# Query features in two halves, the hidden activations scaled on ScalarE alone, and a new order of weight subtractions on VectorE, in a one-core graph layer with experts

## The reference

```python
xn = layernorm(x)
x = x + gnn(xn, edges, W, b) + mix(xn, W_qkv, W_proj, b_proj, proj_mat)
x = x + ffn(layernorm(x), gate_w, ..., fc1_w, fc1_b, ln_w, ln_b, fc2_w, fc2_b)

# mix, for each of 12 heads; q, k, v are 625 x 64, proj_mat is 266 x 64
dd = (q / 64**.25) @ proj_mat.T
q1 = 266**-.5 * (exp(dd - |q|**2 / 16 - dd.max(row)) + 1e-4)     # k1: max over all of k
out = (q1 @ (k1.T @ v)) / (q1 @ k1.sum(0))

# ffn: expert 0 takes every token, each token has up to 3 of the others
h = gelu(xf @ fc1_w[e] + fc1_b[e])                 # 768 -> 1536
h = (h - mean) * rsqrt(var + 1e-5) * ln_w[e] + ln_b[e]
y = h @ fc2_w[e] + fc2_b[e]                        # 1536 -> 768
out = sum over e of combine[:, e] * y
```

## Time and profile before

| | |
|---|---|
| median of 3 runs | 1316.48 us (1313.85 to 1317.22) |
| the profiled execution | 1310.28 us |
| its span in the trace | 1308.6 us |
| mean granted clock of TensorE | 0.981 |
| TensorE busy | 1229.3 us, 94% |
| VectorE busy | 847.8 us, 65% |
| ScalarE busy | 665.0 us, 51% |
| GpSimd busy | 245.9 us, 19% |

### The profile page before, as it was taken

The page is one execution under the profiler, slowest core; times in us unless marked ns, Lnnn a source line. Parts: engine busy times, 40 slices in busy tenths (PEclk is TensorE's granted clock), DMA queues, the critical chain, the costliest instruction groups (busy, mean ns, idle before and its releaser), DMA issues.

```text
span 1308.6 us, 22128 instructions
## 1 busy us (share of the span) xinstructions
PE 1229.3 (94%) x7041; PEld 1092.1 (83%) x7069; DVE 847.8 (65%) x1465; ACT 665.0 (51%) x990; POOL 245.9 (19%) x184
## 2 busy tenths in 40 slices
PE   4899999999997989999999999999999999999985
PEld 3899998998585766789888889988889988889875
DVE  5676666606426855666378686675686698755993
ACT  3313233326614641442466677375577576666853
POOL 1000000003004010005323242121252243213301
PEclk7999999999997999999999999999999999999998
DMA  9100000000005033310686668356659786576944
GB/s 324 40 1 1 1 1 1 1 1 24 2 1 184 2 121 105 109 24 14 194 302 207 223 232 320 108 222 208 214 218 321 250 313 221 174 264 221 336 161 111
DMA packets 55395, 188.97 MB, mean 144 GB/s; under 512 B 7626, under 2 KB 8260, under 8 KB 55346
## 3 DMA queue, kind: packets, MB, share of 16 engines
q1 hardware_dynamic: 47858, 170.07, 35.0%
q0 software_dynamic: 6448, 17.91, 6.7%
q10 hardware_dynamic: 1040, 0.33, 0.1%
HBM read 176.70 MB, written 14.51 MB: 146 GB/s over the span
## 4 chain that ended last, share of the span: by engine, by line
PE 70%; DVE 13%; issue 5%; DMA 4%; DVEq 3%; ACT 3%; ACTq 1%; SPq 0%; POOL 0%; POOLq 0%
PE bank L1812 19%; PE bank L1796 16%; PE bank L1523 7%; PE bank L1611 4%; PE bank L1593 4%; DMA w1raw<-in_L_ffn_fc_w 3%; PE bank L1633 3%; PE bank L1646 2%; DVE w1lo L505 2%; DVEq L519 2%; DVE w2lo L505 2%; PE bank L1665 2%; PE bank L1780 2%; PE bank L1692 2%; PE bank L1733 2%
## 5 line engine op out<-in xcount | busy, mean ns | idle before, releaser
L505 DVE TENSOR_TENSOR w2lo<-w2raw,w2hi 128x1536 fp32r<-128x1536 f32 x96 | 165.6, 1754 | 40.8 <-ACT w2hi L492 40.4
L492 ACT ACTIVATE w2hi<-w2raw 128x1536 fp32r<-128x1536 f32 x96 | 142.2, 1507 | 96.1 <-DMA w2raw<-in_L_ffn_fc_w 83.7
L1812 PE MATMUL bank<-w2hi,hthi 128*128 128x384 f32 x624 | 162.6, 341 | 11.0 <-DVE htlo L1070 10.3
L1812 PE MATMUL bank<-w2lo,hthi 128*128 128x384 f32 x624 | 159.5, 336 | 0.0
L1812 PE MATMUL bank<-w2hi,htlo 128*128 128x384 f32 x624 | 159.2, 336 | 0.0
L492 ACT ACTIVATE w1hi<-w1raw 128x1536 fp32r<-128x1536 f32 x96 | 139.2, 1507 | 34.2 <-DMA w1raw<-in_L_ffn_fc_w 34.2
L1523 PE MATMUL bank<-ohd,ohs 125*125 125x313 bf16 x825 | 129.5, 305 | 20.9 <-DVE ohd L845 19.7
L505 DVE TENSOR_TENSOR w1lo<-w1raw,w1hi 128x1536 fp32r<-128x1536 f32 x80 | 136.9, 1778 | 7.6 <-ACT w1hi L492 7.6
L745 POOL DMA_INDIRECT out<-ysb,sidx x27 | 88.8, 3288 | 281.3 <-issue 241.2
L1796 PE MATMUL bank<-w1hi,xthi 128*128 128x512 f32 x486 | 139.7, 396 | 0.0
L1796 PE MATMUL bank<-w1lo,xthi 128*128 128x512 f32 x486 | 136.9, 390 | 0.0
(11 more groups left out here) (306 smaller groups left out, 2019.5 us busy)
## 6 DMA issues: line engine op xcount, KB each, us to landing
w1raw<-in_L_ffn_fc_w SPq DMA_DIRECT2D x96, 768.0 KB, 6.8
w2raw<-in_L_ffn_fc_w SPq DMA_DIRECT2D x96, 768.0 KB, 6.3
wg<-in_L_gnn_W SPq DMA_DIRECT2D x1, 2304.0 KB, 13.7
wv<-in_L_mix_W_qkv SPq DMA_DIRECT2D x1, 2304.0 KB, 20.0
wk<-in_L_mix_W_qkv SPq DMA_DIRECT2D x1, 2304.0 KB, 24.8
wq<-in_L_mix_W_qkv SPq DMA_DIRECT2D x1, 2304.0 KB, 24.5
out<-xs SPq DMA_DIRECT2D x5, 375.0 KB
xn_dram<-xn SPq DMA_DIRECT2D x5, 375.0 KB
```

The source lines that it names most:

```text
L492: act.activation(unit(w2hi if second else w1hi, second, u), unit(w2raw if second else w1raw, second, u), ACT.Copy).then_inc(w2_hi if secon ...
L505: eng.tensor_tensor(unit(w2lo if second else w1lo, second, u), unit(w2raw if second else w1raw, second, u), unit(w2hi if second else w1hi, ...
L1812: last = pe.matmul(y_ps[s][:, 0:384], a[:, c, :], w[:, c, 384 * s:384 * s + 384], start=c == 0 and k == 0, stop=False)
```

## The change

Ten edits in the programs of the engines:

1. VectorE's `hidden_scale` is gone; ScalarE scales all 12 chunks. The semaphore `v_scaled_act` goes, `v_scaled` is ScalarE's.
2. In the expert loop, VectorE subtracts w2 unit 3 before `hidden_low(j)`, w2 units 4 and 5 behind it, and w1 units 4 and 5 of the block that step j's `fc1` works on behind those (`with_first(dve, j - 1, ...)`). Units 1 to 3 stay in the step before, mixed with w2 units 0 to 2.
3. `q_features` works on six heads at a time; the first half of tile 0 comes after head 7 of the `kv` copies. TensorE waits for half a tile at a time.
4. The tail of the query features is transposed before pair 3, and its product closes each group of heads where it opened it; TensorE no longer waits for its own last product there.
5. The key features of the last tile come before the last messages of the graph part, and TensorE waits for key features tile by tile.
6. The five bias pieces are all done after tile 3 and within tile 4.
7. Most of GpSimd's constants are written after the last graph product, the rest after the last `kv`.
8. The first layer output is stored before the loads of w2 units 3 to 5, and units 4 and 5 are loaded after the last stores.
9. `project_out(2)` comes before `turn_xn2(0)`.
10. w2 unit 4 of expert 0 is subtracted before `normalise(1)`.

```diff
@@ VectorE, expert loop
             with dve.Fori(FIXED, end) as j:
-                hidden_scale(j, entry(dve, EXPERT, j - 1, E - 1))
-                with_second(dve, j, low(3, 4))
+                with_second(dve, j, low(3))
                 hidden_low(j)
-                with_second(dve, j, low(5))
+                with_second(dve, j, low(4, 5))
+                with_first(dve, j - 1, low(4, 5))
                 normalise(j)
                 x_low(j + 1)
-                with_first(dve, j, low(1, 2, 3, 4, 5))
-                with_second(dve, j + 1, low(0, 1, 2))
-            hidden_scale(end, entry(dve, EXPERT, end - 1, E - 1))
-            with_second(dve, end, low(3, 4))
+                with_first(dve, j, low(1, 2))
+                with_second(dve, j + 1, low(0, 1))
+                with_first(dve, j, low(3))
+                with_second(dve, j + 1, low(2))
+            with_second(dve, end, low(3))
             hidden_low(end)
-            with_second(dve, end, low(5))
+            with_second(dve, end, low(4, 5))
+            with_first(dve, end - 1, low(4, 5))
             normalise(end)
-            hidden_scale(nb, E - 1)
@@ ScalarE
-            def hidden_scale(j, e, first=SCALE_BY_ACT):
+            def hidden_scale(j, e):
 
                 act.wait_ge(h_turned, j)
-                for c in range(first, FC):
+                for c in range(FC):
                     last = act.activation(hid[:, 128 * c:128 * c + 128], tr_ps[c // 4][:, 128 * (c % 4):128 * (c % 4) + 128],
                                           ACT.Identity, scale=lnw[:, bass.ds(e, 1), c], bias=lnb[:, bass.ds(e, 1), c])
-                last.then_inc(v_scaled_act, 1)
+                last.then_inc(v_scaled, 1)
@@ VectorE, query features and bias pieces
-            def q_features(i):
-                for h in range(H):
+            def q_features(i, g):
+                heads = slice(6 * g, 6 * g + 6)
+                for h in range(6 * g, 6 * g + 6):
                     taken(dve, ("ddq", i, h))
-                main = q1[i % 2][:, :, 0:MAIN]
+                main = q1[i % 2][:, heads, 0:MAIN]
@@
-                    if p == 4 and i + 1 < NT:
-                        q_features(i + 1)
-                    if p == 5:
-                        bias_part(i)
+                    if p in (2, 4) and i + 1 < NT:
+                        q_features(i + 1, p // 4)
+                    if i == NT - 1 and p in (0, 1, 3):
+                        bias_part((1, 3, None, 4)[p])
@@
+                if i == NT - 2:
+                    bias_part(0)
@@ VectorE, key features
+            for i in range(NT - 1):
+                add_messages(i)
+                k_features(i)
+            k_features(NT - 1)
+            add_messages(NT - 1)
@@ TensorE
                 for i in range(NT):
+                    if g == 0:
+                        pe.wait_ge(k1_ok, i + 1)
@@
                 if p % 3 == 2:
-                    filled(last, ("o", i, g))
-                    done(pe, ("o", i, g))
-                    pe.sem_inc(q1t_used, 1)
-                else:
-                    last.then_inc(q1t_used, 1)
+                    taken(pe, ("tail", i))
+                    filled(pe.matmul(ps[0:TP, 0:6 * (HD + 1)], q1tt[:, i % 2, :], kvt[:, 6 * g:6 * g + 6, :], start=False, stop=True), ("o", i, g))
@@
-                pe.wait_ge(q1_ok, i + 1)
+                pe.wait_ge(q1_ok, 2 * i + 1)
                 turn_pair(i, 0)
@@
+                    if p == 2:
+                        pe.wait_ge(q1_ok, 2 * i + 2)
@@
             project_out(1)
+            project_out(2)
             turn_xn2(0)
-            project_out(2)
```

More of the change, by code:

```diff
@@ L332, in gps_kernel @@
         for i in range(NT):
-            groups([("q1t", i, 0), ("tail", i)], R6)
+            groups([("q1t", i, 0)], R6)
             for p in range(H // 2):
@@ L336, in gps_kernel @@
                     groups([("q1t", i, p + 1)], R6)
+                if p == 2:
+                    groups([("tail", i)], R6)
                 if i + 1 < NT:
@@ L599, in _ @@
                 sp.wait_ge(x1_ok, i + 1)
+                sp.dma_start(out[TP * i:TP * i + TP, :], xs[:, i, :]).then_inc(st_x1[i], 16)
                 if i == NT - 1:
-                    for u in range(3, C):
-                        load(True, 0, u)
-                sp.dma_start(out[TP * i:TP * i + TP, :], xs[:, i, :]).then_inc(st_x1[i], 16)
+                    load(True, 0, 3)
                 sp.wait_ge(xn2_ok, i + 1)
                 sp.dma_start(xn2_dram[TP * i:TP * i + TP, :], xn2[:, i, :]).then_inc(st_xn2[i], 16)
+            for u in (4, 5):
+                load(True, 0, u)
             sp.wait_ge(st_slot, 16 * TOPK * NT)
@@ L707, in _ @@
                                    base=-32 * g, pattern=[[-1, E], [0, 128]], channel_multiplier=1).then_inc(sel_ok, 1)
+            done(pool, ("kv", H - 1))
+            pool.memset(bl[:, :], 0.0).then_inc(bl_zero, 1)
+            pool.memset(padrow[0:1, :], 0.0).then_inc(pad_ok, 1)
             pool.wait_ge(bsplit_ok, 1)
@@ L955, in _, with add_messages @@
             dve.wait_ge(x_biased, NT + 1)
-            for i in range(NT):
+            def add_messages(i):
                 for s in range(2):
@@ L961, in _, with k_features @@
                                                      op0=ALU.mult, op1=ALU.add), ("gnn", i, s))
+            def k_features(i):
                 dve.wait_ge(kexp_ok, i + 1)
@@ L1058, in _ @@
             STEPS = 11
-            def hidden_scale(j, e, chunks=SCALE_BY_ACT):
-                dve.wait_ge(h_turned, j)
-                for c in range(chunks):
-                    last = dve.tensor_scalar(hid[:, 128 * c:128 * c + 128], tr_ps[c // 4][:, 128 * (c % 4):128 * (c % 4) + 128],
-                                             lnw[:, bass.ds(e, 1), c], lnb[:, bass.ds(e, 1), c], ALU.mult, ALU.add)
-                last.then_inc(v_scaled, 1)
             def hidden_low(j, hi=hthi, lo=htlo):
@@ L1187, in _ @@
             scores()
+            split_lo(dve, True, 0, range(4, 5))
             normalise(1)
-            split_lo(dve, True, 0, range(4, 5))
             x_low(2)
@@ L1377, in _ @@
                         take_pair(i, p + 1)
+                    if p == 2:
+                        take_tail(i)
                     for r in AHEAD[p] if i + 1 < NT else ():
@@ L1681, in attend @@
                 g = p // 3
-                if p % 3 == 0:
-                    ps = fill(pe, ("o", i, g))
-                    taken(pe, ("tail", i))
-                    pe.matmul(ps[0:TP, 0:6 * (HD + 1)], q1tt[:, i % 2, :], kvt[:, 6 * g:6 * g + 6, :], start=True, stop=False)
-                ps = bank[plan[("o", i, g)][0]]
+                ps = fill(pe, ("o", i, g)) if p % 3 == 0 else bank[plan[("o", i, g)][0]]
                 taken(pe, ("q1t", i, p))
@@ L1876, in turn_last @@
                 pe.wait_ge(v_scaled, end)
-                pe.wait_ge(v_scaled_act, end)
                 turn_h(nb)
```

40 lines of the change are left out of this document (17 added, 23 removed).

## The result

The changed kernel takes **1387.6 us** (median of four runs, 1384.3 to 1393.5) against 1315.2 (four runs): ratio **1.0555**, 95% interval 1.0514 to 1.0596. It is 5.5% slower. The forecast was 1367 with a range of 1345 to 1389: the direction and the mechanism are right, the size is 21 us short. The profiled execution of the changed kernel took 1386.6 us, 76.3 more than that of the kernel before (1310.3), where +50.8 was forecast.

A forecast was written before the change was run, and what follows sets the result against it. TensorE, busy 94%, was taken as the bound. Loop +65.6 and first half with end -14.8 gave +50.8 on the profiled 1310.3, so 1361; the median's 6.2 made it 1367 us, range 1345 to 1389.

The forecast's parts named there:

- The mechanism: Expert loop: w1 units 4 and 5, wanted sooner, queue behind later-wanted `htlo` on in-order VectorE; some 15 TensorE waits on `w1lo`.
- T+9.67: T is a loop step's start on TensorE; w1 unit 4 of `fc1` was forecast to begin costing at T+9.65.
- Small steps: Eight expert-change steps with w1 units alone: unit 4 ready at T+11.2, TensorE loses 1.55 us each, 12.4 in all.
- Large steps: Seven steps with w1 and w2 units: TensorE loses 7.4 to 9.9 us each, taken as 8.0, 56 in all.
- s-T: Delay from step start to ScalarE's scaling start in the seven steps: 1.73 us least, 4.24 worst, 3.1 average.
- The clock: TensorE's lower clock behind the seven waits of 8 us costs 1.5 us each, 10.5 in all.
- First half: Before the expert loop: shorter feature and projection waits against costlier bias pieces, -15.5 us in sum.
- Removed waits: Expert loop: the seven old `htlo` waits go, -10.3 us, with -3.0 of their clock.
- The rule weighed: ScalarE's scaling by the skill's fixed-cost figure: an estimated 0.25 us per chunk, not 0.343; sum 17 lower, 1350.
- no small wait was hidden: Rival in the expert loop: eight small waits hidden, seven large stay at 6 to 7 us; 1344 to 1350, 14%.
- the cascade: Rival: later w1 use delays loads, roundings and scaling, small waits slow the clock; 20 to 30 us more, 1385 to 1397, 11%.
- unit 4 is never late: Rival in the expert loop: w1 unit 4 comes in time, only the removals count; 1288 us, 4%.

The follow-up runs named there:

- Experiments 1: Changed kernel with VectorE's w1 units 4 and 5 moved ahead of the w2 unit and `htlo` in the same step: 1285.5 us, ratio 0.9774 to the kernel before.
- 3: Changed kernel with all five VectorE w1 units in the step before, as in the old order; ScalarE keeps all scaling: 1291.7 us, ratio 0.9824.
- 2: Changed kernel with w1 units 4 and 5 still behind `htlo`, but ahead of w2 units 4 and 5: 1355.4 us.
- 5: Kernel before with VectorE's new order of weight units alone, VectorE still scaling four of twelve chunks: 1372.8 us, ratio 1.0451.
- experiment 7: Changed kernel with 34 useless matmuls in TensorE's queue ahead of w1 unit 4 in steps with both weight changes: 1384.1 us.
- Experiment 8: Changed kernel with 50 useless matmuls in TensorE's queue ahead of w1 unit 4 in steps with both weight changes: 1374.1 us.
- experiments 6: Kernel before with the expert loop's change alone (VectorE's new order and ScalarE's scaling), first half as before: 1397.1 us, ratio 1.0638.
- 10: Changed kernel with w1 units 4 and 5 ahead of `htlo`, bias pieces spread over tiles, last w2 unit 5 behind the norm: 1287.1 us, ratio 0.9800.

## Why the prediction was right, and where it was short

- **The mechanism** held as written: `w1lo` as releaser of `fc1`, 15 times, seven large and eight small, `htlo` gone, 27.73 us for a step without a change of expert. Unit 4 begins to cost at T+9.67 (forecast 9.65). Experiments 1 and 3 take the waits away; 2 and 5 move them in the way and near the amounts that it gives (the large ones by 3.0 where 3.4 was expected, the small ones by 1.25 where 1.4 was).
- **Small steps**, 1.55 each: mis-sized, 2.43. The step "start of `htlo`, + 1.67" took VectorE's operations as back to back. Between `htlo` and `w1lo` lies the skipped block of the w2 units, with 0.70 us of "issue"; experiment 2 takes it from between them and the wait is 0.78 shorter. The restart adds 0.3, and `htlo` came 0.1 sooner than forecast.
- **Large steps**, 8.0 each: 9.2. I had 8.8 from the mean of ScalarE's starts and took 8.0, since pauses of TensorE should let the transfers catch up. They did not: s-T is 2.35 to 4.52 in the seven, 3.3 on average, and ScalarE's roundings of w2 still wait for their data ahead of the scaling. From s on the chain is as forecast: in step 25, 3.78 + 5.7 makes 9.5, and the wait is 9.39. The choice within the bounds was wrong. The mean held in the bounds (7.4 to 9.9); the longest single one, a wait of 10.12 and 0.3, did not.
- **The clock**, 1.5 for each large wait: 2.1. I took it from two rows, behind waits of 2.2 and 3.4 us. It varies from 1.3 to 2.8, and not with the length of the wait: 1.3 behind 8.44 us in the changed kernel, 2.8 behind 5.44 in experiment 2, and 1.6 to 2.7 behind the 2.8 to 4.4 of experiment 7. Experiment 8 confirms the mean. Leaving the small waits without it was nearly right: one of eight had it.
- **First half**, -15.5: -9.7 in this profile. Part of the difference was lost to the clock between 190 and 236 us, where nothing was changed. The same first half in the profile of version 1 started step 4 at 614.15, a gain of 13.2, which is 3.5 more. The bias pieces cost 4.65 (a wait of 3.66 where it was 1.29, and 5.67 for the transposes behind it where they took 3.39), where the term was 4.1.
- **Removed waits**, -13.3: -15.1, with their restarts of nearly 0.3 each.
- **The rule weighed**: the chunks came every 0.343 us again (twelve in 4.12 us, from 1281.13 to 1285.25, where the next operation starts), as the earlier trace rows said. The sum by the Trainium skill's figure (VectorE: DVE Perf Modes, The TRN2 errata) would have missed by 38 us.
- **Rivals**: no small wait was hidden. The number falls into what I gave for the cascade (1385 to 1397, 11%), and part of it came true: s-T averaged 3.3. But nothing grew from step to step, since steps without a change of expert take 27.73 behind a large one too, and one small wait of eight slowed the clock. The case "unit 4 is never late" is what experiment 1 made of it: it gave 1288, and that version runs in 1285.5.
- **The median**: I added 6.2 us, because the profiled execution of the kernel before lay that far below its median. The changed kernel's profiled execution lies 1 us below its own; such an offset does not carry over. Without it the forecast would have been 27 us short, not 21: a third of the effect was missing. That the measured time still lies in the range, 1.4 us below its end, owes something to this offset.

## What to carry to other kernels

An in-order queue should be sorted by when the result is wanted, and an operation that itself waits for something late belongs behind whatever it could hold up: VectorE was only 59% busy, and the two units fitted into the 6.7 us for which it stood waiting. When work is moved to another engine, see what is queued behind the operation that it makes later; the same move cost nothing in one order and 24 us in the other. And price a wait of TensorE with what follows it, here 0.3 us of restart and, behind the waits of 2.8 to 10 us in the loop, some 2 us of lower clock.

## What the runs showed of the hardware that I had not expected

- **VectorE and GpSimd hold each other up.** A subtraction of 128x1536 takes 1.75 us on VectorE and 3.5 on GpSimd. Where the two overlap, VectorE's takes up to 5.08 us. In version 1, VectorE and then GpSimd:

```profile
1209.49 6.75 DVE L505 TENSOR_TENSOR w2lo<-w2raw,w2hi 128x1536 fp32r<-128x1536 f32 x2
...
1211.05 3.56 POOL L505 TENSOR_TENSOR w1lo<-w1raw,w1hi 128x1536 fp32r<-128x1536 f32 x1 [1.44 <-PE bank L1789]
```

  The second of the two started at 1211.16 and ended 1.6 after GpSimd's end, as if it had begun only then. It goes the other way too: where VectorE's subtractions are under way first, GpSimd's takes up to 5.04 us in the changed kernel (at 1039.87, beside VectorE's from 1038.11 on). In the loop of the kernel before, no VectorE subtraction took more than 1.76 and none of GpSimd's more than 3.53: the two never met. The Trainium skill (GPSIMD Engine Reference, Specifications) says that GpSimd shares its SBUF interfaces with VectorE, and that instructions with two SBUF inputs contend; the trace agrees.
- **Which waits cost the clock.** It fell behind all seven waits of 8 to 10 us, behind the seven of 4.3 to 7.2 in experiment 2, behind the six of 2.8 to 4.4 that the first filling left, behind one of the eight of 2.1 in the changed kernel, two of eight in experiments 6 and 7 and three of eight in experiment 8, and behind none of 1.33 (experiment 2) or 0.86 (experiment 5). Filling only a part of a wait did not keep the clock up.
- **A skipped conditional block** costs VectorE 0.70 us in the trace, where one that is entered costs nothing that shows: in the large step `htlo` starts at 1289.59 and the first w2 unit inside its block at 1291.26, 1.67 later, as between any two. The Trainium skill (Advanced Engine Details and Errata, Control Flow Timing) has some 0.11 us for a compare-and-branch; the trace shows more, and no run here tells where it goes.
- **The clock is not the same in two executions of the same code.** At 190 us, behind a wait of 2.17 in both, the granted clock is 0.83 from 190 to 200 in the changed kernel and 1.00 in version 1, whose program is the same up to there; with the stretch from 216 on that makes some 3 us by the start of step 4. The same wait stands in all 14 profiles of this case, and the clock is 0.83 behind it in four (the changed kernel, 2, 7 and 10) and 1.00 in ten. A difference of this size between two profiles needs no cause in the edit.
